# A two-layer sampling convolution on one core: from four gathered and five dense taps to three gathered and six dense

## What is computed

```python
offset = _conv2d(x, w_p, b_p, padding=1)
m = jax.nn.sigmoid(_conv2d(x, w_m, b_m, padding=1))
...
x_off = g_lt * gather(q_lt_x, q_lt_y) + g_rb * gather(q_rb_x, q_rb_y) + ...
x_off = x_off * m
return _conv2d(x_off, w_conv, None, stride=KS, padding=0)
```

## Time and profile before

| | us |
|---|---|
| median of 3 runs | 538.03 |
| lowest and highest run | 537.27, 539.29 |
| span of the profiled execution | 702.7 |
| first gather of the second layer in it | 198.29 |

### The profile page before, as it was taken

One profiled execution on the slowest core, in us unless ns is written; L12 is line 12 of the kernel. 1 busy time (PEld: TensorE's weight loads), 2 busy tenths in 40 slices (PEclk: granted clock), 3 DMA queues, 4 the chain that ended last, 5 costly groups with the idle time before them and its releaser, 6 DMA issues.

```text
span 702.7 us, 10708 instructions
## 1 busy us (share of the span) xinstructions
PE 543.3 (77%) x3862; PEld 294.6 (42%) x3862; DVE 392.4 (56%) x876; ACT 147.7 (21%) x292; POOL 326.1 (46%) x336
## 2 busy tenths in 40 slices
PE   4838898794853788868888788887878888776777
PEld 3515555563721334333444333343434334433344
DVE  3346768684444655556555455665555666544564
ACT  3202211112520221222222121222112122121201
POOL 2363656520053555544555544455554455455440
PEclk9999999997695899997899988899898879889869
DMA  4995787830580111111211361111111111111110
GB/s 111 276 210 128 159 169 123 144 69 3 166 222 27 36 50 43 51 52 44 66 50 54 72 80 37 31 39 40 40 42 35 34 35 38 38 38 42 33 35 11
DMA packets 41924, 52.24 MB, mean 74 GB/s; under 512 B 16766, under 2 KB 32930, under 8 KB 41872
## 3 DMA queue, kind: packets, MB, share of 16 engines
q1 hardware_dynamic: 31464, 30.19, 19.9%
q0 software_dynamic: 10240, 20.99, 11.2%
q10 hardware_dynamic: 168, 0.34, 0.2%
HBM read 34.80 MB, written 8.72 MB: 62 GB/s over the span
## 4 chain that ended last, share of the span: by engine, by line
PE 53%; another core or an unknown queue 17%; DVE 12%; issue 12%; DMA 2%; ACT 2%; DVEq 1%; SPq 0%; POOL 0%; ACTq 0%
PE ps_later L1178 9%; PE ps_pair L1178 8%; PE ps_raw L980 5%; PE ps_x L1191 5%; PE ps_raw L1152 3%; DVE vprod L1620 3%; PE ps_x L1045 3%; PE ps_x L1201 3%; DVE vlast L1620 2%; PE ps_o L993 2%; PE ps_later L1023 2%; PE ps_pair L1045 1%; DVE prod L1819 1%; DMA shared<-positions 1%
## 5 line engine op out<-in xcount | busy, mean ns | idle before, releaser
L614 POOL DMA_INDIRECT got<-table,idx x320 | 318.8, 996 | 296.6 <-DVE prod L1819 147.6
L1620 DVE TENSOR_TENSOR vprod<-ps_pair,rhat 128x704 f32<-128x704 f32 x64 | 57.0, 890 | 71.6 <-remote 31.4
L1620 DVE TENSOR_TENSOR vprod<-ps_later,rhat 128x704 f32<-128x704 f32 x64 | 56.7, 885 | 42.1 <-PE ps_pair L1178 25.3
L1191 PEld LDWEIGHTS ps_x<-early,vprod 128*128 128x128 f32 x384 | 49.8, 163 | 42.4 <-issue 33.6
L1191 PE MATMUL ps_x<-early,vprod 128*128 128x128 f32 x384 | 65.4, 315 | 0.6 <-DVE vlast L1631 0.6
L1178 PE MATMUL ps_later<-columns_of,shared 64*64 64x352 f32 x320 | 43.6, 554 | 19.5 <-DVE vlast L1620 11.3
L1178 PE MATMUL ps_pair<-columns_of 64*64 64x352 f32 x320 | 41.9, 557 | 20.6 <-DVE vlast L1620 10.3
L1802 DVE TENSOR_TENSOR samples<-shared,vprod 128x800 f32<-128x800 f32 x48 | 47.1, 986 | 11.9 <-PE ps_x L1045 4.8
L1628 DVE TENSOR_TENSOR vprod<-vprod 128x640 f32<-128x640 f32 x64 | 52.5, 821 | 1.2
L1152 PE MATMUL ps_raw<-conv_out,later 128*128 128x512 f32 x64 | 44.5, 780 | 10.9 <-issue 10.2
L1178 PE MATMUL ps_pair<-columns_of,shared 64*64 64x352 f32 x320 | 39.5, 526 | 15.2 <-DVE vlast L1620 5.9
(11 more groups left out here) (216 smaller groups left out, 722.9 us busy)
## 6 DMA issues: line engine op xcount, KB each, us to landing
shared<-positions SPq DMA_DIRECT2D x24, 440.0 KB
xn<-xq SPq DMA_DIRECT2D x52, 132.0 KB, 3.9
got<-table,idx POOLq DMA_INDIRECT x320
table<-trow SPq DMA_DIRECT2D x9, 234.0 KB
table<-trow SPq DMA_DIRECT2D x2, 1024.0 KB, 4.5
out<-ysumT SPq DMA_DIRECT2D x64, 16.0 KB
columns_of<-table SPq DMA_DIRECT2D x2, 512.0 KB
table<-trow SPq DMA_DIRECT2D x1, 936.0 KB
```

Source lines behind the costliest of these rows:

```text
L614: pool.indirect_dma_start(into[t][:, s * P:(s + 1) * P], None, tab, bass.IndirectOffsetOnAxis(ap=idx[:, slot, k:k + 1], axis=0),).then_inc ...
L1191: nc.tensor.matmul(bank[:, P:2 * P], vprod[:, t % 2, r, :], idn[:], start=(r == 0), stop=(r == HALF - 1), is_transpose=True)
L1620: nc.vector.tensor_tensor(dst, ps_dense[pair_number(0, t, pair) % 2][:].rearrange("p (d n) -> p d n", d=2)[:, :, 0:WROWS * C].rearrange("p ...
```

## The change

Taps 0 to 2 are gathered and taps 3 to 8 are dense, three pairs for every tile. A group then has 12 gathers and 12 pairs. `vlast` gets its own half for each tile, twice as wide, with a fold for every tile, and TensorE turns it with four transposes per tile in place of two. The third spread becomes as wide as the others. `prod` keeps four slots per corner, of which the fourth is zeroed once; `prod` and `got` keep their sizes. DVE's order changes: the fold of pairs 0 and 1 is put ahead of the product of pair 2, and TensorE waits for the two folds separately. Pair 2 no longer waits for the turning of tile T.

```diff
-GT = 4
+GT = 3
 DT = 9 - GT
 BLOCKS1 = 3
-PAIRS = 10
+PAIRS = 3 * TT
...
-        vlast = sb("vlast", [P, 2, WROWS, C])
+        vlast = sb("vlast", [P, 2, WROWS, 2 * C])
...
-            return range(3 if t % 2 == 0 else 2)
+            return range(3)
...
-                N = GPIX if k < 2 else GPIX // 2
-                nc.scalar.activation(chat[u][:, k, 0:N], ps_raw[:, 0:N], ACT.Abs).then_inc(chat_abs, 1)
+                nc.scalar.activation(chat[u][:, k, :], ps_raw[:, :], ACT.Abs).then_inc(chat_abs, 1)
...
-                if k < 2:
-                    last = nc.tensor.matmul(ps_raw[:, :], spr[:, k, :], conv_out[g % 2][:], start=True, stop=True)
-                else:
-
-                    for h in range(2):
-                        last = nc.tensor.matmul(
-                            ps_raw[W * h:W * (h + 1), 0:2 * P], spr[:, k, W * h:W * (h + 1)],
-                            conv_out[g % 2][:].rearrange("p (a t n) -> p a t n", t=2, n=P)[:, :, h, :],
-                            start=True, stop=True)
+                last = nc.tensor.matmul(ps_raw[:, :], spr[:, k, :], conv_out[g % 2][:], start=True, stop=True)
...
-                pe.wait_ge(v_added, additions_done(tile // TT, t))
+                pe.wait_ge(v_added, 2 * tile + 1)
...
-                for a in range(0, KEPT, CORNERS):
+                pe.wait_ge(v_added, 2 * tile + 2)
+                for a in range(0, KEPT, 2):
                     last = nc.tensor.matmul(bank[:, 2 * P:3 * P],
-                                            vlast[:, t % 2, a:a + CORNERS, :].rearrange("p w c -> p (w c)"), idn[:],
-                                            start=(a == 0),
-                                            stop=(a + CORNERS == KEPT), is_transpose=True)
+                                            vlast[:, t % 2, a:a + 2, :].rearrange("p w c -> p (w c)"), idn[:],
+                                            start=(a == 0), stop=(a + 2 == KEPT), is_transpose=True)
                 last.then_inc(v_turned, 1)
+                if tile == 0:
+                    pe.wait_ge(prod_clear, 1)
...
+                if not (first and t < 2):
+                    dve.wait_ge(v_turned, tile - 1)
                 for pair in pairs_of(t):
-                    if not (first and t < 2):
-                        if pair == 0:
-                            dve.wait_ge(v_turned, tile - 1)
-                        elif pair == 2:
-                            dve.wait_ge(v_turned, tile)
...
                     between(pair)
+                    if pair == 1:
+                        dve.wait_ge(v_read, n + 1)
+                        half = WROWS - HALF
+                        nc.vector.tensor_tensor(vprod[:, t % 2, 0:half, :], vprod[:, t % 2, 0:half, :],
+                                                vprod[:, t % 2, HALF:WROWS, :], ALU.add).then_inc(v_added, 1)
                 dve.wait_ge(v_read, pairs_done(g, t))
-                half = WROWS - HALF
-                nc.vector.tensor_tensor(vprod[:, t % 2, 0:half, :], vprod[:, t % 2, 0:half, :],
-                                        vprod[:, t % 2, HALF:WROWS, :], ALU.add).then_inc(v_added, 1)
-                if t % 2 == 0:
-                    nc.vector.tensor_tensor(vlast[:, :, 0:WROWS - KEPT, :], vlast[:, :, 0:WROWS - KEPT, :],
-                                            vlast[:, :, KEPT:WROWS, :], ALU.add).then_inc(v_added, 1)
+                nc.vector.tensor_tensor(vlast[:, t % 2, 0:WROWS - KEPT, :], vlast[:, t % 2, 0:WROWS - KEPT, :],
+                                        vlast[:, t % 2, KEPT:WROWS, :], ALU.add).then_inc(v_added, 1)
...
-                    prod[:, t % 2, :].rearrange("p (k s c) -> p s k c", k=CORNERS, c=C),
-                    got[t].rearrange("p (s k c) -> p s k c", s=GT, c=C),
+                    prod[:, t % 2, :].rearrange("p (k s c) -> p s k c", k=CORNERS, c=C)[:, 0:GT],
+                    got[t][:, 0:GT * P].rearrange("p (s k c) -> p s k c", s=GT, c=C),
...
+            nc.vector.memset(prod[:].rearrange("p t (k s c) -> p (t k) s c", s=CORNERS, c=C)[:, :, GT, :],
+                             0.0).then_inc(prod_clear, 1)
```

More of the change, by code:

```diff
@@ L111 @@
              bias0=1, inner=1)
-LATER = dict(fold_proj=P, conv_w1=4 * 32, grid1=27, grid2=27, w4=9 * C, steps1=WROWS, spread=SPREADS * P, wd0=C, wd=C,
+LATER = dict(fold_proj=P, conv_w1=4 * 32, grid1=27, grid2=27, w4=9 * C, steps1=WROWS, spread=SPREADS * P, wd0=C, wd=C, wlast=C,
              gamma=1, beta=1, bias1=1)
@@ L216, in build @@
                 for flat in (sb("prow", [P, Q * PT0 * C])[:], v_flat[:, 1616:1616 + Q * PT0 * C])]
-        prod = sb("prod", [P, 2, GT * P])
+        prod = sb("prod", [P, 2, CORNERS * P])
         columns_of = sb("columns_of", [P, B * XROWS * C + SPREADS * GPIX])
@@ L404, in pairs_done @@
             return pair_number(g, t, len(pairs_of(t)))
-        def additions_done(g, t):
-            return 6 * g + sum(2 - k % 2 for k in range(t + 1))
         def is_far(eng):
@@ L832, in column_weights @@
                 act.wait_ge(spread_mm, SPREADS * g + k + 1)
-                N = GPIX if k < 2 else GPIX // 2
-                nc.scalar.activation(chat[u][:, k, 0:N], ps_raw[:, 0:N], ACT.Abs).then_inc(chat_abs, 1)
+                nc.scalar.activation(chat[u][:, k, :], ps_raw[:, :], ACT.Abs).then_inc(chat_abs, 1)
                 act.wait_ge(chat_abs, SPREADS * g + k + 1)
-                nc.scalar.activation(chat[u][:, k, 0:N], chat[u][:, k, 0:N], ACT.Relu, bias=1.0,
+                nc.scalar.activation(chat[u][:, k, :], chat[u][:, k, :], ACT.Relu, bias=1.0,
                                      scale=-1.0).then_inc(chat_in, 1)
@@ L1175, in interpolate @@
                     for h in range(2):
-                        at, tap, slot = (t + h, 8, t // 2) if pair == 2 else (t, GT + 2 * pair + h, t)
-                        top = (g % GB) * GROWS + 2 * at + tap // 3 - 1 + r
+                        tap = GT + 2 * pair + h
+                        top = (g % GB) * GROWS + 2 * t + tap // 3 - 1 + r
                         nc.tensor.matmul(ps_dense[n % 2][W * r:W * (r + 1), h * GPIX:h * GPIX + WROWS * C],
-                                         chat[g % 2][W * h:W * (h + 1), pair, slot * P + W * r:slot * P + W * (r + 1)],
+                                         chat[g % 2][W * h:W * (h + 1), pair, t * P + W * r:t * P + W * (r + 1)],
                                          xcol[b][W * h:W * (h + 1), top * C:(top + WROWS) * C],
@@ L1606, in weigh_rows @@
                 tile = g * TT + t
+                if not (first and t < 2):
+                    dve.wait_ge(v_turned, tile - 1)
                 for pair in pairs_of(t):
-                    if not (first and t < 2):
-                        if pair == 0:
-                            dve.wait_ge(v_turned, tile - 1)
-                        elif pair == 2:
-                            dve.wait_ge(v_turned, tile)
                     n = pair_number(g, t, pair)
                     dve.wait_ge(v_mm, 4 * n + 4)
[L1615 to L1619, removed]
+                    dst = (vprod[:, t % 2].rearrange("p w (d c) -> p d w c", c=C)[:, 2 * pair:2 * pair + 2]
+                           if pair < 2 else vlast[:, t % 2].rearrange("p w (d c) -> p d w c", c=C))
                     nc.vector.tensor_tensor(
@@ L2105, in _lay_out @@
                  grid1=grid1, grid2=grid2, rows=rows, rooms=rooms, steps=np.broadcast_to(steps, (P, SIDE)), steps1=steps1,
-                 spread=spread, conv_fold=conv_fold, w4=w4, wd0=wd0, wd=wd,
+                 spread=spread, conv_fold=conv_fold, w4=w4, wd0=wd0, wd=wd, wlast=wlast,
                  gamma=around(f["L0_conv_bn_gamma"]), beta=around(f["L0_conv_bn_beta"]),
```

15 lines of the change are left out of this document (8 added, 7 removed).

## The result

The changed kernel takes **557.12 us**, median of 4 runs (554.97 to 561.61). The kernel before has 538.66 beside it, median of 4 (537.27 to 546.75). The ratio is 1.0331, with a 95% interval of 1.0281 to 1.0381: slower by 18.5 us. The run of 546.75 belongs to a slower state that some executions show, and the ratio leaves such runs out. The forecast of 559 is 1.9 us too high, and the side was right.

A forecast was written before the change was run, and what follows sets the result against it. POOL's gathers were taken to hold each second-layer group at 20.7 us before, and PE at 22.0 after: 16 x (22.0 - 20.7) = +21 on 538 gives 559 us, range 547 to 572, chance 0.45.

The forecast's parts named there:

- What bounds it before: In the second layer POOL's gathers were taken as the limit, 20.7 us a group, with PE close behind.
- PE's sum: PE's work for one second-layer group, summed: 18.5 us before (up to 20.4), 21.3 after (up to 23.4).
- The value taken: PE's group after the change, taken as 22.0 us between 21.3 and 23.4, nearer the lower end.
- The sum: Over the second layer's groups: 16 x (22.0 - 20.7) = +21 us, giving 559; the ends give +10 and +43.
- The reordering: Fold moved ahead of the third product: PE waits 0 to 0.3 us, at tile 3, if at all.
- DVE: DVE's work for one group goes from 17.0 to 19.1 us, below PE, so it hides.
- The recorded execution: Separate forecast for a profiled execution of the changed kernel: 702.7 + 16 x (2.8 - 2.4) = 709 us.
- PE's steps shorter than recorded: Unrecorded PE steps are shorter, PE stays below POOL's old time, DVE sets the pace: -22, 516 us; chance 0.22.
- PE holds the group already before: PE holds the group at 20.4 us before, so the added 2.76 counts in full: +44, 582 us; chance 0.18.
- No change, by a clock that recovers: PE's waits and slow steps make its group 21.5 us before, 21.3 after: -3, 535 to 541 us; chance 0.15.

The follow-up runs named there:

- The second record: The kernel before, unchanged, profiled once more: median 538.48 us, ratio 0.9996; the record's span is 536.4 us.
- three gathers: The kernel before with only three of the four gathers of each second-layer tile issued, other engines' work unchanged: 510.54 us, ratio 0.9474.
- the added spread: The kernel before with one more wide spread matmul on PE in each group, its result written over: 539.86 us, ratio 1.0011.

## Why the prediction was right

**What bounds it before.** POOL, at 20.7 in a group, was an inference against the record, in which POOL waits for DVE. The second record shows it: 21.0 by its gathers, 20.81 by PE's 13 groups, and POOL without a wait. The sum that seemed to confirm it, 198.29 + 331 = 529 beside a median of 538, fitted in part by luck, since 198.29 came from the stretched record; in the second one it is 190.36. Four gathers, 5.0 us, were predicted to go from POOL; after, it waits some 2 us at a time instead.

**PE's sum.** Before, 18.5 was summed and 18.80 measured with three gathers. After, 21.3 was summed; the group that starts at 380.92 takes 402.64 - 380.92 = 21.72 from first spread to first spread, of which 0.50 is the wait, so 21.22. By parts: the 8 transposes 0.82 (0.88 predicted), the turned tile 1.65 (1.66), the spread 381.97 - 380.92 = 1.05 (1.06).

**The value taken.** 22.0 was taken between 21.3 and 23.4, and 22.06 measured over 13 groups. The size holds, the reason given for it does not, so the closeness is luck: there are no gaps of 10% on PE. What lies between the bare sum and the mean are two other things. One is the wait of 0.50 at tile 3. The other was not in the sum: in the first groups PE also turns parts of the input, two times four transposes in a group. The changed kernel in that stretch:

```profile
268.68 1.10 PE L1147 MATMUL ps_raw<-conv_out,later 128*128 128x512 f32 x2
...
280.37 0.72 PE L912 MATMUL ps_raw<-early,xq 128*128 128x128 f32 x4
...
290.44 0.73 PE L912 MATMUL ps_raw<-early,xq 128*128 128x128 f32 x4
291.90 1.10 PE L1147 MATMUL ps_raw<-conv_out,later 128*128 128x512 f32 x2
```

That group takes 291.90 - 268.68 = 23.22, 1.50 more than the 21.72 later. From 222.90 to 337.48 the five groups take 114.58 against 5 x 21.72 = 108.60, so this is 6 us of the kernel's time. Under POOL's pace such work was covered.

**The sum.** 16 x 1.3 = 21 was forecast; 16 x (22.06 - 20.81) = 20.0 follows from the two records, their spans differ by 555.1 - 536.4 = 18.7, and the runs by 18.5. The means hold one odd group each way: 25.50 in the record of before (see the third rival) and 20.18 at the end of the changed kernel's 13.

**The reordering.** It was taken as 0 to 0.3 us of waiting for PE in a group, at tile 3, because DVE would reach the end of its work there too late. The place was right; the size and the cause were off. The 0.50 at tile 3 is not DVE being late: the product for which PE waits had waited for PE, as DVE's row in the changed kernel shows.

```profile
375.31 0.89 DVE L1602 TENSOR_TENSOR vlast<-ps_later,rhat 128x704 f32<-128x704 f32 x1 [0.56 <-PE ps_later L1166]
```

Pair 2 is written to `ps_later` at 374.34, its product ends at 376.20, and the pair after next, which needs that buffer, starts at 376.25. With two buffers and three pairs in a row the round trip through DVE shows; put other work of PE between them, and it is hidden (the kernel with the end of the convolution first). And the fold ahead of the product is a gain: with the fold behind, 13 groups are 2.67 us longer in the records, 0.21 each or 3.4 in 16, and the runs give 4.6 with overlapping intervals. The prediction priced the move as a small loss: it named what the transposes gain by it and put no number to that, and it did not look at the next tile, whose products the fold delays when it stands behind.

**DVE.** 19.1 was summed, and it works 169.98 us in 200, 0.85 of the time, or 18.7 in a group of 22.06. It stays hidden, as said.

**The recorded execution.** This step failed, though the forecast for the timed runs doesn't use it. 709 us was forecast for a record of the changed kernel, and it is 555.1. The step took the idle stretches of the earlier trace rows for something that goes with each gather in any record. The second record of before has as many gathers and none of these stretches, and the kernel with a fourth gather has the same groups as the change. Why the first record held 166 us more is not settled; nothing in these runs repeats it. The rule weighed against it, that TensorE and ScalarE never wait on anyone (the Trainium skill, "SBUF — State Buffer", section "Who interferes with whom"), agrees with these later records: with four more gathers in a group TensorE is busy 195.51 us in 200 as without them, and ScalarE 63.36 against 63.54. By that rule the stretches were no matter of ports, or belonged to the recording. Its other consequence in the prediction, that fewer gathers then give TensorE nothing, holds for the change (558.86 with the fourth gather) but not for the kernel before, where TensorE waited for the data and not for a port.

**Rivals.** *PE's steps shorter than recorded* falls: 21.22 against 21.3. *PE holds the group already before* falls by the kernel with three gathers (28 us faster) and by the added spread (nothing). *No change, by a clock that recovers* falls: in the second record of before the clock from 225 to 425 us is 0.98, so there was little to recover. It fell in one of the 13 groups, after PE had waited 3.24 us for a gathered product: the group from 320.88 to 346.38 takes 25.50 at 0.87, the next one 18.78, and POOL's gathers go on 0.3 apart through both. In the change the clock is 1.00 there, and it is slower all the same.

## What to carry to other kernels

Count each engine's work for one period from rows without waits, and take the largest as the bound, even where the record shows that engine waiting; then have it recorded again. Moving work from the bound engine pays up to the slack of the engine that receives it (here 1.7 us in a group, 2.76 were moved), so size the move to that slack: moving two of the four gathers, in a form that adds no transposes on PE, turned a loss of 18.5 us into a gain of 8.4. That run changed the size and the form together, so it doesn't say how much is owed to either. And a sum for one period should be looked up in several periods, since some carry work of another stage.

## What the runs showed of the hardware that was not expected

The granted clock at the start of the second layer is at either level in records of one program, with the same instructions ahead of it: from the end of one convolution (line 989) to the first spread PE's starts lie 187.92 - 184.13 = 3.79 us apart in the record of the change that stayed at 2.4 GHz, and 187.61 - 183.82 = 3.79 in the one that fell to 1.2 GHz. That first spread takes 1.10 us in the one and 1.87 in the other, the next 1.13 and 2.07. What decides between the two levels stays open. From the start of that spread to the first spread of the group after the next the first record takes 222.90 - 187.92 = 34.98 us and the second 227.36 - 187.61 = 39.75, 4.8 more, about as much as the order of the fold is worth, so that two kernels some 4 us apart can't be ranked by one record of each.
